# Rounds of two batches with seven block products in place of eight, and the program written out, in a two-layer graph network on one Trainium2 core

## The reference

```python
h = jnp.maximum(_layernorm(x, axis=-1), 0.0)
x = x + (einsum('nm,bmo->bno', adj, einsum('bnc,co->bno', h, weight)) + bias)
h = jnp.maximum(_layernorm(x, axis=-1), 0.0)
input = h                       # layer 1, in_matrix = out_matrix = adj
for _ in range(5):
    m_in = einsum('nm,bmd->bnd', adj, h); m_out = m_in; av = concatenate([m_in, m_out])
    u3 = h @ u3_w.T + u3_b
    z  = sigmoid(av @ w3_w.T + w3_b + u3)
    r  = sigmoid(av @ w4_w.T + w4_b + u3)
    hv = tanh(av @ w5_w.T + w5_b + (r * h @ u5_w.T + u5_b))
    h  = (1.0 - z) * h + z * hv
x = x + h
```

## Time and profile before

| | |
|---|---|
| median of 3 runs | 1581.13 us |
| profiled execution, its own time | 1581.27 us |
| its span, from first to last instruction | 1579.4 us |
| PE busy | 98% of the span |
| DVE, ACT, POOL busy | 62%, 44%, 22% |
| mean granted TensorE clock | 0.994 |

### The profile page before, as it was taken

The page is one execution under the profiler, slowest core; times in us unless marked ns, Lnnn a source line. Parts: engine busy times, 40 slices in busy tenths (PEclk is TensorE's granted clock), DMA queues, the critical chain, the costliest instruction groups (busy, mean ns, idle before and its releaser), DMA issues.

```text
span 1579.4 us, 23033 instructions
## 1 busy us (share of the span) xinstructions
PE 1550.6 (98%) x7471; PEld 720.8 (46%) x7471; DVE 983.8 (62%) x1823; ACT 701.2 (44%) x1090; POOL 347.2 (22%) x817
## 2 busy tenths in 40 slices
PE   6899999999999999999999999999999999999997
PEld 4444444444444444444444444444444444444443
DVE  7675558655576556765567556675556755576556
ACT  3244434444444444444434444354443444344444
POOL 6230042300613006130062101530024300330000
PEclk8999999999999999999999999999999999999999
DMA  4121113211131111311113111221112211122111
GB/s 150 40 46 35 27 28 84 51 27 34 21 99 34 33 33 26 94 33 34 27 47 78 35 27 27 66 66 27 33 33 53 66 33 33 27 52 48 34 27 54
DMA packets 214238, 71.87 MB, mean 46 GB/s; under 512 B 208192, under 2 KB 209088, under 8 KB 214208
## 3 DMA queue, kind: packets, MB, share of 16 engines
q1 hardware_dynamic: 212480, 70.83, 19.4%
q10 hardware_dynamic: 1728, 0.66, 0.2%
HBM read 13.24 MB, written 8.39 MB: 14 GB/s over the span
## 4 chain that ended last, share of the span: by engine, by line
PE 95%; DVE 2%; DMA 1%; SPq 0%; issue 0%; ACT 0%; POOL 0%; DVEq 0%; POOLq 0%; ACTq 0%
PE ps_m L559 62%; PE ps_u L581 6%; PE ps_u L585 6%; PE ps_u L583 6%; PE ps_v L581 4%; PE ps_v L585 4%; PE ps_v L583 4%; DVE adj_lo L872 1%; DMA adj_in<-in_adj_dram 1%; PE ps_x L604 0%; PE ps_x L606 0%; PE ps_x L605 0%; POOL x_in L455 0%; SPq L393 0%; DMA h_lo<-nh_lo 0%
## 5 line engine op out<-in xcount | busy, mean ns | idle before, releaser
L559 PE MATMUL ps_m<-adj_hi,nh_hi 128*128 128x512 f16 x1280 | 485.1, 379 | 2.6 <-ACT nh_hi L732 2.6
L559 PE MATMUL ps_m<-adj_lo,nh_hi 128*128 128x512 f16 x1280 | 485.1, 379 | 0.0
L559 PE MATMUL ps_m<-adj_hi,nh_lo 128*128 128x512 f16 x1280 | 485.1, 379 | 0.0
L756 ACT ACTIVATE m_hi<-ps_m 128x512 f16<-128x512 f32 x192 | 113.2, 590 | 341.3 <-PE ps_m L559 341.3
L969 DVE SCALAR_TENSOR_TENSOR m_lo<-ps_m,m_hi 128x512 f16<-128x512 f32 x192 | 131.9, 687 | 203.6 <-ACT m_hi L756 203.3
L978 DVE SCALAR_TENSOR_TENSOR cand<-cand,h 128x512 f32<-128x512 f32 x160 | 107.9, 691 | 186.2 <-ACT cand L762 186.2
L309 POOL TENSOR_TENSOR mean<-stats 128x8 f32<-128x8 f32 x23 | 7.4, 322 | 871.7 <-DVE stats L908 871.7
L559 PEld LDWEIGHTS ps_m<-adj_hi,nh_lo 128*128 128x128 f16 x1280 | 125.3, 98 | 151.0
L559 PEld LDWEIGHTS ps_m<-adj_hi,nh_hi 128*128 128x128 f16 x1280 | 125.3, 98 | 150.6 <-issue 3.3
L559 PEld LDWEIGHTS ps_m<-adj_lo,nh_hi 128*128 128x128 f16 x1280 | 125.3, 98 | 147.2
L751 ACT ACTIVATE h_hi<-h 128x512 f16<-128x512 f32 x158 | 97.4, 630 | 209.3 <-DVE h L990 209.3
(11 more groups left out here) (136 smaller groups left out, 2050.2 us busy)
## 6 DMA issues: line engine op xcount, KB each, us to landing
x_in<-in_x_dram SPq DMA_DIRECT2D x16, 512.0 KB, 3.4
out_dram<-y SPq DMA_DIRECT2D x16, 512.0 KB, 2.7
adj_in<-in_adj_dram SPq DMA_DIRECT2D x8, 512.0 KB, 7.4
nh_hi<-h_hi SPq DMA_TRANSPOSE x128, 2.4
nh_lo<-h_lo SPq DMA_TRANSPOSE x128, 2.4
h_hi<-nh_hi SPq DMA_TRANSPOSE x32, 2.4
h_lo<-nh_lo SPq DMA_TRANSPOSE x32, 2.5
n_hi<-h_hi SPq DMA_TRANSPOSE x30, 2.4
```

The costliest lines, as they stand in the source:

```text
L559: last = nc.tensor.matmul(ps_m[half][:, :], a[slot][:, k, :], b[:, k, cols(half)], start=(k == 0 and n == 0), stop=(k == BLOCKS - 1 and n ...
L756: nc.scalar.activation(m_hi[:, cols(half)], ps_m[half][:, :], ACT.Copy, scale=M_SCALE).then_inc(m_hi_done, 1)
```

## The change

Batches go in groups of four, a slot holds two. A round is two batches, a and b, times the adjacency. The state of a slot has four quarters of 512 nodes: q = 0 and 1 are the halves of a, 2 and 3 those of b. Taken as a matrix of 2 x 2 blocks, its product with the adjacency (2 x 2 blocks too) takes seven block products of 12 matmuls each (4 blocks x 3 parts), A0, S1, S2, A1, S3, B1, S4, in place of eight:

- The left operands of A0, A1, B1 are quarters of the state as they are. S1 to S4 are sums: s1 = b0 + b1, s2 = s1 - a0, s3 = a0 - b0, s4 = a1 - s2 (`sum_state` on DVE, four additions; then hi and lo by `round_s` on ACT and `rest_s` on DVE, and 14 DMA transposes a step in place of 8 for two batches).
- The right operands are seven blocks `t_hi`, `t_lo`, made once at the start: four are sums of blocks of the adjacency (`sum_rows` on DVE), and 28 units of 4 transposes of 128 x 128 are made where there were 16.
- A0, S2, S3 and B1 add up in one bank, `ps_a`. Between them ACT copies the sum reached (`evacuate`, three a round), and DVE adds another bank to the copy (`sum_m`, three a round). `bank_free` holds PE at S2, S3 and B1 until the copy is made. Hi and lo of the result follow as before (`round_m`, `rest_m`), per quarter, in the order 0, 3, 2, 1.

The turned operands have one set of buffers for both slots (`nx_hi`, `nx_lo`): a transpose into a place waits for the product of the running round that reads it. ACT applies the layer norm (`normalise`, 16 activations of 128 x 128, in two lots of 8 or one of 16), POOL only makes the moments; `sum_n` on DVE makes the sums for the first product of a layer. New states and their roundings go two quarters (1024 elements) at a time (`side`). There are 48 rounds, 40 steps and 8 of layer 0, and no loops in the program.

```diff
+    K_A0, K_S1, K_S2, K_A1, K_S3, K_B1, K_S4 = range(7)
+    STEP_ORDER = (K_A0, K_S1, K_S2, K_A1, K_S3, K_B1, K_S4)
+    LAYER_ORDER = (K_A0, K_S1, K_S2, K_S3, K_A1, K_B1, K_S4)
+    START_ORDER = (K_A0, K_A1, K_S1, K_S2, K_S3, K_B1, K_S4)
...
+    QUARTERS = (0, 3, 2, 1)
+    POS = {0: 0, 3: 1, 2: 2, 1: 3}
...
+        P_BANK = {K_A0: ps_a, K_S1: ps_c, K_S2: ps_a, K_A1: ps_b, K_S3: ps_a, K_B1: ps_a, K_S4: ps_c}
...
+        def all_rounds(layer, step):
+            layer(0, 0)
+            layer(0, 1)
+            for p in range(GROUPS):
+                for t in range(END):
+                    step(p, t, 0)
+                    step(p, t, 1)
+                if p + 1 < GROUPS:
+                    layer(p + 1, 0)
+                step(p, END, 0)
+                step(p, END, 1)
+                if p + 1 < GROUPS:
+                    layer(p + 1, 1)
...
+        T_ROWS = {K_A0: A11, K_A1: A12, K_S4: A22, K_S1: A11, K_S2: t2_rows, K_S3: A21, K_B1: A12}
+        T_ORDER = (K_A0, K_A1, K_S4, K_S1, K_S2, K_S3, K_B1)
...
-                        pe.wait_ge(*lo_ready[k // HB])
-                    for n, (a, b) in enumerate(((a_hi, adj_hi), (a_hi, adj_lo), (a_lo, adj_hi))):
-                        last = nc.tensor.matmul(ps_m[half][:, :], a[slot][:, k, :], b[:, k, cols(half)],
...
+            def block_product(k, a_hi, a_lo):
+                opens, o = k in OPENS, P_BANK[k]
+                for j in range(HB):
+                    for n, (a, b) in enumerate(((a_hi, t_hi), (a_hi, t_lo), (a_lo, t_hi))):
+                        last = nc.tensor.matmul(o[:, :], a[:, PLACE[k], j, :], b[:, k, j, :],
+                                                start=(opens and j == 0 and n == 0), stop=(j == HB - 1 and n == 2),
+                                                skip_group_check=not opens)
+                last.then_inc(prod_done, 1)
+            def bank_free(g, k):
+                if k == K_A0 and g > 0:
+                    pe.wait_ge(m_lo_done, 4 * (g - 1) + 1 + POS[2])
+                elif k == K_S1 and g > 0:
+                    pe.wait_ge(c_done, 3 * g)
+                elif k == K_S2:
+                    pe.wait_ge(evac_done, 3 * g + 1)
+                elif k == K_S3:
+                    pe.wait_ge(evac_done, 3 * g + 2)
+                elif k == K_B1:
+                    pe.wait_ge(evac_done, 3 * g + 3)
+                elif k == K_S4:
+                    pe.wait_ge(c_done, 3 * g + 2)
...
+                step_product(p, t, slot, K_A0)
+                if before is None:
+                    v_product(s - 1, 2)
+                    v_product(s - 1, 1)
+                else:
+                    if s > 0:
+                        pe.wait_ge(cand_ready, 4 * s)
+                        pe.wait_ge(z_ready, 4 * s)
+                    for q in QUARTERS:
+                        layer_out(*before, q)
+                step_product(p, t, slot, K_S1)
+                step_product(p, t, slot, K_S2)
+                step_product(p, t, slot, K_A1)
+                step_product(p, t, slot, K_S3)
+                if t == 0:
+                    for k in range(2):
+                        pe.wait_ge(first_in[slot][k], 4 * 16 * (p + 1))
+                else:
+                    pe.wait_ge(h16_lo_done, 2 * (s - 1))
+                if before is not None:
+                    pe.wait_ge(x1_ready, 4 * n_layer(*before) + 4)
...
+                u_product(slot, 0)
+                u_product(slot, 3)
+                step_product(p, t, slot, K_B1)
+                r_product(g, 0)
+                r_product(g, 3)
+                step_product(p, t, slot, K_S4)
+                u_product(slot, 2)
+                z_product(s, 0)
+                r_product(g, 2)
+                z_product(s, 3)
+                pe.wait_ge(z_ready, 4 * s + 1)
+                u_product(slot, 1)
+                r_product(g, 1)
+                v_product(s, 0)
+                z_product(s, 2)
+                v_product(s, 3)
+                z_product(s, 1)
...
+                for q in quarters:
+                    for b in range(HB * q, HB * (q + 1)):
+                        last = nc.scalar.activation(ysc[:, b, :], source[:, b, :], ACT.Relu,
+                                                    bias=shift[slot][:, b:b + 1], scale=rstd[slot][:, b:b + 1])
...
+            def evacuate(g, s, n, order=STEP_ORDER):
+                k, q = ((K_A0, 0), (K_S2, 1), (K_S3, 3))[n]
+                act.wait_ge(prod_done, made(g, k, order))
...
+                nc.scalar.activation(m_sum[:, q, :], ps_a[:, :], ACT.Copy).then_inc(evac_done, 1)
...
+                if before is None:
+                    before_t = t if slot == 1 else t - 1
+                    if first1:
+                        round_n(p, 1, 1, 2)
+                    candidate(s - 1, 3)
+                    evacuate(g, s, 0)
+                    candidate(s - 1, 2)
+                    candidate(s - 1, 1)
+                    round_h(s - 1, 1 - slot, 0)
+                    if first1:
+                        round_n(p, 1, 1, 3)
+                    if steps_ahead(p, t, slot, 2, 1):
+                        normalise(p + 1, 0, 0, range(2))
+                    if steps_ahead(p, t, slot, 3, 0):
+                        round_n(p + 1, 0, 0, 0)
+                        round_n(p + 1, 0, 0, 1)
+                    if steps_ahead(p, t, slot, END, 1):
+                        normalise(p + 1, 1, 0, range(2))
+                    round_h(s - 1, 1 - slot, 1)
+                    evacuate(g, s, 1)
+                    if before_t < END:
+                        round_s(p, before_t, 1 - slot, 0)
+                    if steps_ahead(p, t, slot, 2, 1):
+                        normalise(p + 1, 0, 0, range(2, 4))
+                    if steps_ahead(p, t, slot, END, 1):
+                        normalise(p + 1, 1, 0, range(2, 4))
+                    if before_t < END:
+                        round_s(p, before_t, 1 - slot, 1)
                 else:
+                    if t == 0:
+                        round_n(p, 1, 0, 3)
+                    evacuate(g, s, 0)
+                    evacuate(g, s, 1)
+                    if t == END:
+                        normalise(p + 1, 0, 1)
+                evacuate(g, s, 2)
                 round_m(g, 0)
+                round_m(g, 3)
+                if steps_ahead(p, t, slot, 3, 1):
+                    round_n(p + 1, 0, 0, 2)
+                if steps_ahead(p, t, slot, END, 0):
+                    round_n(p + 1, 0, 1, 0)
+                    round_n(p + 1, 0, 1, 1)
+                round_m(g, 2)
+                sigmoid_r(s, 0)
+                sigmoid_r(s, 3)
+                if t == 0 and slot == 0:
+                    normalise(p, 1, 1, range(2))
+                round_rh(s, 0)
+                round_rh(s, 3)
                 round_m(g, 1)
+                sigmoid_z(s, 0)
+                sigmoid_r(s, 2)
+                if t == 0 and slot == 0:
+                    normalise(p, 1, 1, range(2, 4))
+                sigmoid_z(s, 3)
+                sigmoid_r(s, 1)
+                round_rh(s, 2)
+                candidate(s, 0)
+                round_rh(s, 1)
+                sigmoid_z(s, 2)
+                sigmoid_z(s, 1)
+                if steps_ahead(p, t, slot, 3, 1):
+                    round_n(p + 1, 0, 0, 3)
+                if steps_ahead(p, t, slot, END, 0):
+                    round_n(p + 1, 0, 1, 2)
+                    round_n(p + 1, 0, 1, 3)
+                if t == 0 and slot == 0:
+                    round_n(p, 1, 1, 0)
+                    round_n(p, 1, 1, 1)
...
+            def sum_m(g, q, order=STEP_ORDER):
+                k, bank_in, evac = {0: (K_A1, ps_b, 1), 3: (K_S3, ps_c, 3), 1: (K_S4, ps_c, 2)}[q]
+                dve.wait_ge(evac_done, 3 * g + evac)
+                dve.wait_ge(prod_done, made(g, k, order))
+                nc.vector.tensor_add(m_sum[:, q, :], bank_in[:, :], m_sum[:, q, :]).then_inc(c_done, 1)
...
+            def sum_state(e, s, slot, k):
+                a0, a1, b0_, b1 = (h[slot][:, q, :] for q in range(4))
+                s1, s2, s3, s4 = (state_sum[:, q, :] for q in range(4))
+                if k == 0:
+                    dve.wait_ge(h_ready, 2 * s + 2)
+                    nc.vector.tensor_add(s1, b0_, b1).then_inc(s_done, 1)
+                elif k == 1:
+                    dve.wait_ge(s_done, 4 * e + 1)
+                    nc.vector.tensor_sub(s2, s1, a0).then_inc(s_done, 1)
+                elif k == 2:
+                    nc.vector.tensor_sub(s3, a0, b0_).then_inc(s_done, 1)
+                else:
+                    dve.wait_ge(s_done, 4 * e + 2)
+                    nc.vector.tensor_sub(s4, a1, s2).then_inc(s_done, 1)
...
+                    before_t = t if slot == 1 else t - 1
+                    sums = before_t < END
+                    e = n_sum(p, before_t, other)
+                    if first1:
+                        rest_n(p, 1, 1, 2)
+                    new_state(s - 1, other, 0)
```

(77 more changed lines are left out.)

1273 lines of the change are left out of this document (697 added, 576 removed).

## The result

The changed kernel takes 1630.2 us (median of 4 runs, 1627.5 to 1630.8), the kernel before beside it 1581.1: a ratio of 1.031, 95% interval 1.029 to 1.033. It is slower by 49 us; 1566 were predicted, 15 less than before.

A forecast was written before the change was run, and what follows sets the result against it. PE's matmuls were taken as the bound: 1409.8 us of work + start 58.9 + first steps 54.0 + turns 23.0 + ordinary steps 1.7 + clock 5.1 + end 12.0 = 1564.5 span, forecast 1566; 8-in-10 range 1530 to 1594.

The forecast's parts named there:

- the ordinary step: Steps away from a group's turn: PE full, 31.06 us each, VectorE's chain just in time, 1.7 us lost over 24 steps.
- rival 2: VectorE's chain in ordinary steps is longer than 13.8 us: 27 us more, 1593 us; chance 0.16.
- the first step of slot 1: At each group's start, one VectorE chain up to the lo of quarter 3 makes PE lose 12.0 us.
- rival 1: First steps cost a group 4 us, not 13.5, and a turn 5, not 7.65: 1520 us; chance 0.18.
- rival 4: Fetching the longer PE program costs 0.5 us per 16 KB: 27 us, 1593 us in all; chance 0.02.
- second layer round 0.4; transposes and loads of 1 MB fit in it: At each of three group turns, the second layer-0 round loses PE only 0.4 us.
- the layer norm of step 2 at 0.9: At each of three group turns, the next group's layer norm delays the third copy by 0.9 us.
- The activations: Layer norm activations of 128 x 128 on ScalarE take 0.30 us each, bounds 0.285 and 0.375.
- The clock: After the wait before B1, PE runs at low clock: about 1.7 us, 5.1 in three; bounds 0 and 10.
- The first step of slot 0: At each group's start, layer norm activations delay the gate that frees a bank: PE waits 1.5 us.
- The start: First step begins at 97.9 us with 39.0 of PE work before it: costs 58.9 us, bounds 50 and 66.
- activations at 0.41: Rival: layer norm activations of 128 x 128 cost 0.41 us each, giving 1585 us; chance 0.07.

The follow-up runs named there:

- the first h: Changed kernel with 112 of 128 columns left out of the two VectorE additions making slot 1's first state, in three of four groups: 1621.2 us.
- the first experiment: Changed kernel with GpSimd's bias addition left out on 15 of the 16 blocks of x: 1599.2 us, 1.011 of the kernel before.
- Bias in pieces: Changed kernel with GpSimd's whole bias added in four additions of 512 elements, each started where VectorE waits, in place of one of 2048: 1606.3 us.
- the run with 32 columns: Changed kernel with 96 of 128 columns left out of each layer norm activation, but for the first two lots: 1621.3 us.
- outputs late: Changed kernel, all work kept: bias in four pieces, statistics early, layer norm activations spread, previous group's outputs in VectorE's last waits of slot 0's first step: 1564.7 us.

## Why the prediction was wrong

**Right.** What PE saves; the ordinary step and VectorE's chain in it (31.08 for 31.13, rival 2 out); the first step of slot 1 as one chain on VectorE (11.7 for 12.0), whose law the first h confirmed in two of three groups, and with it that the low clock behind its A0 is covered; so rival 1, first steps that cost far less, is out; the first layer round; the end. The gap of 5.4 us "issue" at the start ends 0.2 us behind ScalarE's copy, which stood behind 16 activations; the only other one (1.7 us, also at the start) ends 0.1 us behind a rest on VectorE. No ordinary step has one, with 57 packets of code for 16: rival 4 is out.

**Wrong, by cause.**
- The step that failed is "second layer round 0.4; transposes and loads of 1 MB fit in it", and with it the layer norm of step 2 at 0.9. GpSimd's bias addition is in no term of the prediction; it stood at nothing. It stops a VectorE operation for as long as it lasts: 7.2 us and not 0.4 in the second layer round, 5.3 and not 0.9 in step 2, 31.0 in all by the first experiment. Bias in pieces, with all of the work kept, got 23.9 of them back. The trace of before had it. Its addition of 1024 elements, and VectorE beside it, once with two inputs from SBUF and once with one from PSUM (POOL, DVE, POOL, DVE):
```profile
298.96 2.57 POOL L445 TENSOR_TENSOR x_in<-x_in,b_rows 128x1024 f32<-128x1024 f32 x1 [0.18 <-POOL y L437]
```
```profile
299.24 2.85 DVE L1087 TENSOR_TENSOR rh_lo<-rh,rh_hi 128x512 f16<-128x512 f32 x1
```
```profile
609.94 2.35 POOL L445 TENSOR_TENSOR x_in<-x_in,b_rows 128x1024 f32<-128x1024 f32 x1 [0.18 <-POOL y L437]
```
```profile
610.96 0.69 DVE L969 SCALAR_TENSOR_TENSOR m_lo<-ps_m,m_hi 128x512 f16<-128x512 f32 x1 [0.27 <-ACT m_hi L756]
```
  2.85 us for 0.68 at seven places, where PE had slack to hide it. The change made the addition twice as long, and put it beside operations of 1024 and 512 elements of which both inputs lie in SBUF, in a chain without slack. The Trainium skill says it ("SBUF — State Buffer", SBUF: two separate sides): a VectorE operation with two SBUF inputs and a GpSimd operation that reads SBUF exclude each other for the whole instruction. The rows agree: VectorE is held (5.53 us for 1.22), GpSimd is held (4.55 for 0.23), and with one input in PSUM neither is (0.69 and 0.23).
- The activations: 0.386 us where I took 0.30, and above my upper bound of 0.375. I chose the copy's price because "Relu and the copy need no table function"; no run shows that a table function is what a gate costs more (0.66 for 0.57). In the code that gate has bias and scale by pointer, and so has this activation; the copy has the scale alone. The upper bound came from the gate, which reads PSUM and not SBUF; why it lies 0.01 too low is not shown. By the run with 32 columns the difference is worth 8.9 us. The Trainium skill has a form for this ("ScalarE: Activation LUTs", What ACT_TABLE_LOAD costs): 186 ns and 0.833 ns a column, 93 for each pointer, less 93 of overlap back to back; worked out from it, an estimate of 0.386 us for 128 columns and 0.306 for 32. The traces have 0.386, and 0.304 in the run with 32 columns.
- The clock, 5.1 us with a bound of 10. In 178 places two matmuls of 512 columns start about 0.43 us apart and not 0.22; together 36.0 us. I priced only one wait a group at the low level, the one before B1 (1.7 us; 1.8 to 2.1 measured). The one of 5.4 us in the second layer round fell too (1.4 to 1.7 us), the one of 4.2 us in the first step of slot 0 (1.2 to 1.4), and the waits of step 2 in two of three groups (1.4 to 1.6). How much of the 36.0 is in the time can't be said: behind A0 in the first step of slot 1 it is none, and in the last group of the run with the first h on 16 columns it was 1.8 us (38.59 for 36.83).
- The first step of slot 0, 5.7 us for 1.5: moments at 7.0 us, 14.3 in the trace, since VectorE holds GpSimd in its turn. With them at 9.4, and the activations spread, the pair falls from 79.7 to 77.0.
- The start, 9.8 us late: some 3 are the additions beside the lo of quarter 0 (104.9 and 104.3 with the bias left out or in pieces, for 107.7); the rest was not tried apart.

A rival of mine, activations at 0.41, gave 1585, slower than before. By the runs (8.9 us for the 0.08 between 128 and 32 columns) that price would add some 12 us, an estimate, and give 1578: it would not have turned the sign alone. What turned it was in no rival: an engine with little to do as a hindrance. That outputs late takes 1564.7 us, near the forecast of 1566, bears nothing out: it is another order of the same work, and it lands there by chance.

## What to carry to other kernels

Where a change lengthens or moves an operation of an idle engine, look in the trace of before at what the others do beside it: the same instruction at 0.68 and 2.85 us in one trace is a sign of something that both engines need. Work taken from the bound engine shows in full only where the engines behind it have slack left in that round, so lay out the odd rounds as carefully as the ordinary ones. In this case 65.6 us came back by moving instructions in three queues and splitting one, none by less work: before a change is dropped, its order is to be tried.

## What the runs showed of the hardware that was not expected

- VectorE with both inputs in SBUF and GpSimd stop each other: 5.53 us for 1.22 beside an addition of 4.87, and 4.55 us for 0.23 on GpSimd beside four VectorE operations. With one input in PSUM neither is held (0.69 and 0.23). My expectation that 16-bit inputs do it was too narrow: L1215 reads fp32.
- GpSimd's chain of 23 small operations, most of them dependent, is held again and again: it took 7.1 us while VectorE waited and 14.3 us beside VectorE's operations of 1.2 us.
- Work without use in a wait kept PE at full clock (0.22 apart behind 16 such matmuls, 0.43 without). It was worth nothing where another engine set the end, and the low level came back behind the next wait (3.67 us).
